# Squaring the log on ScalarE for even heads and on GpSimd for odd ones, in a hyperbolic attention kernel

## The reference

```python
q_hyp = _expmap0(qn); k_hyp = _expmap0(kn)
inner = -jnp.einsum('bhti,bhsi->bhts', q_hyp[..., :1], k_hyp[..., :1]) + jnp.einsum('bhtd,bhsd->bhts', q_hyp[..., 1:], k_hyp[..., 1:])
mdot = jnp.maximum(-inner, 1.0 + 1e-06)
dist = jnp.arccosh(mdot)
scores_hyper = -(dist * dist) / curv_k
scores = (1.0 - alpha) * scores_euclid + alpha * scores_hyper
scores = jnp.where(causal[None, None], scores, -jnp.inf)
attn = jax.nn.softmax(scores, axis=-1) * spike_mask
y = jnp.einsum('bhts,bhsd->bhtd', attn, v)
```

## Time and profile before

| | |
|---|---|
| median of 3 runs | 2524.64 us (2520.67 to 2529.24) |
| the profiled execution | 2528.54 us |
| its span, first to last instruction | 2526.8 us |
| mean granted TensorE clock | 0.835 |
| first stage, from about | 100 to 1130 us |

### The profile page before, as it was taken

One profiled execution on the slowest core, in us unless ns is written; L12 is line 12 of the kernel. 1 busy time (PEld: TensorE's weight loads), 2 busy tenths in 40 slices (PEclk: granted clock), 3 DMA queues, 4 the chain that ended last, 5 costly groups with the idle time before them and its releaser, 6 DMA issues. The chain is left out here.

```text
span 2526.8 us, 38830 instructions
## 1 busy us (share of the span) xinstructions
PE 2123.9 (84%) x12343; PEld 1132.9 (45%) x12344; DVE 1605.6 (64%) x3493; ACT 1493.4 (59%) x2762; POOL 613.4 (24%) x638
## 2 busy tenths in 40 slices
PE   4599899989898989994688988888885399999991
PEld 2244444545454444442222322222222288888880
DVE  4576877878787877672566556666652555555556
ACT  1487887888787878882156555565564143333332
POOL 4321314041413232014111122112012133333320
PEclk9677897979897968787689878887777599999995
DMA  1220202121211111100502222452434811111116
GB/s 46 71 64 17 79 18 63 39 59 43 59 43 55 47 51 43 34 9 17 84 18 43 43 51 68 109 143 79 108 108 144 331 67 44 48 44 48 46 38 208
DMA packets 140067, 172.35 MB, mean 68 GB/s; under 512 B 23874, under 2 KB 120339, under 8 KB 137875
## 3 DMA queue, kind: packets, MB, share of 16 engines
q1 hardware_dynamic: 131426, 149.58, 21.3%
q0 software_dynamic: 7488, 20.46, 2.7%
q10 hardware_dynamic: 1008, 0.54, 0.1%
HBM read 105.47 MB, written 65.01 MB: 67 GB/s over the span
## 5 line engine op out<-in xcount | busy, mean ns | idle before, releaser
L1243 DVE TENSOR_REDUCE NM<-sP 128x1 f32<-128x512 f32 x512 | 332.9, 684 | 241.5 <-PE sP L1126 239.6
L1058 ACT ACTIVATE PT<-tP 128x512 f32<-128x512 f32 x512 | 285.7, 604 | 264.9 <-PE tP L1138 263.0
L674 DVE CUSTOM_DVE_ANT_0 YZ<-SeP,YZ 128x512 f32<-128x512 f32 (+3 forms) x512 | 243.5, 487 | 196.4 <-PE SeP L541 179.2
L476 ACT ACTIVATE YZ<-YZ,gsc 128x512 f32<-128x512 f32 (+3 forms) x512 | 325.6, 663 | 69.4 <-DVE YZ L663 69.1
L1489 ACT ACTIVATE H<-hP,B1T 128x256 f32<-128x256 f32 x312 | 127.0, 473 | 271.0 <-PE hP L1568 209.0
L566 PE MATMUL tPa<-ident,YZ 128*128 128x128 f32 x1280 | 258.0, 323 | 1.2 <-ACT PTa L462 0.8
L454 ACT ACTIVATE XL<-mP 128x512 f32<-128x512 f32 (+1 forms) x384 | 204.9, 534 | 63.6 <-PE mP L551 63.3
L462 ACT ACTIVATE PTa<-tPa 128x512 f32<-128x512 f32 (+1 forms) x384 | 207.6, 541 | 41.9 <-PE tPa L572 37.7
L540 PE MATMUL SeP<-STG 48*128 48x512 f16 (+3 forms) x512 | 172.6, 337 | 50.7 <-DVE mn L674 49.5
L663 DVE SCALAR_TENSOR_TENSOR YZ<-YZ,XL 128x1280 f32<-128x1280 f32 x128 | 198.8, 1553 | 21.0 <-ACT YZ L468 19.6
L1126 PE MATMUL sP<-STGb 48*128 48x512 f16 x512 | 171.0, 449 | 46.2 <-DVE NM L1243 36.0
(11 more groups left out here) (301 smaller groups left out, 3994.4 us busy)
## 6 DMA issues: line engine op xcount, KB each, us to landing
STG<-planes_a_scratch SPq DMA_DIRECT2D x512, 32.0 KB, 1.9
X<-in_L_ffn_W SPq DMA_DIRECT2D x32, 512.0 KB, 4.2
weight_planes<-X SPq DMA_DIRECT2D x64, 256.0 KB, 2.5
STGb<-planes_scratch SPq DMA_DIRECT2D x96, 128.0 KB, 6.9
planes_a_scratch<-HI SPq DMA_DIRECT2D x64, 128.0 KB, 1.7
planes_a_scratch<-LO SPq DMA_DIRECT2D x64, 128.0 KB, 1.8
STG<-planes_a_scratch SPq DMA_DIRECT2D x128, 64.0 KB, 2.1
Y<-results_scratch SPq DMA_DIRECT2D x16, 512.0 KB, 8.8
```

Of the source, the lines that this page charges most:

```text
L476: act.activation(w, w, ACT.Square, bias=gsc[:, b % 2, 1, i, hh:hh + 1], scale=gsc[:, b % 2, 0, i, hh:hh + 1]).then_inc(hyp_ready, 1)
L674: dve.tensor_tensor_reduce(out=w, in0=SeP[tc % 2][:, 0:W[i]], in1=w, scale=1.0, scalar=3e38, op0=ALU.add, op1=ALU.min, accum_out=mn[:, h % ...
L1058: act.activation(PT[:, p % 4, par, kt, :], tP[x % 3][:, :], ACT.Exp).then_inc(exp_done, 1)
L1243: dve.tensor_reduce(NM[:, g % 2, col:col + 1], sP[n % 2][:, :], AX.X, ALU.max, negate=True).then_inc(max_done, 1)
```

## The change

Squares of even heads stay on ACT. Those of odd heads become a multiplication of `XL` by itself on POOL, in the same slot and with the same waits, ahead of whatever piece POOL has in that slot. The semaphore `y_ready` becomes two, one for each engine, and Z waits for the one of its head.

```diff
-            y_ready = sem("y_ready")
+            y_even = sem("y_even")
+            y_odd = sem("y_odd")
...
                 def _(pool):
                     for n in range(BEGIN, END):
                         s, t = n // SUB, n % SUB
+                        h = s - 1
+                        if t == 2 and 0 <= h < HEADS and h % 2 == 1:
+                            pool.wait_ge(clamped, h + 1)
+                            if h >= NYZ:
+                                pool.wait_ge(tp_full, 3 * (h - NYZ + 1))
+                            pool.tensor_tensor(YZ[:, h % NYZ, :], XL[:, h % NXL, :], XL[:, h % NXL, :], ALU.mult).then_inc(y_odd, 1)
...
                         h = s - 1
-                        if t == 2 and 0 <= h < HEADS:
+                        if t == 2 and 0 <= h < HEADS and h % 2 == 0:
                             act.wait_ge(clamped, h + 1)
                             if h >= NYZ:
                                 act.wait_ge(tp_full, 3 * (h - NYZ + 1))
-                            act.activation(YZ[:, h % NYZ, :], XL[:, h % NXL, :], ACT.Square).then_inc(y_ready, 1)
+                            act.activation(YZ[:, h % NYZ, :], XL[:, h % NXL, :], ACT.Square).then_inc(y_even, 1)
...
                         if t == 0 and 0 <= h < HEADS:
-                            dve.wait_ge(y_ready, h + 1)
+                            dve.wait_ge(y_odd if h % 2 else y_even, h // 2 + 1)
```

## The result

The changed kernel takes 2596.56 us, the median of 4 executions (2577.43 to 2602.07), against 2523.20 for the kernel before beside it (4, 2520.67 to 2529.24). The ratio is 1.0262 with an interval of 1.0221 to 1.0302: 73 us more, 2.6% slower. I had forecast 2530 and given "slower" 0.35.

What follows compares the result with a forecast made beforehand. PE was taken as near its limit in the hyperbolic attention, ACT often waiting for Z. Losses of 0.4 us a batch over 8 batches (3 us) plus 2 us in the last 20 heads gave +5: 2530 us, range 2512 to 2548.

Steps and rivals of the forecast that it cites:

- slower: Rival, chance 0.35: POOL's square makes Z late with thin cover; 2560 us uncovered in 8 batches, 2542 half covered.
- its rival: Rival "faster", chance 0.20: ACT's relief reaches PE in the hyperbolic attention, giving 10 to 26 us, 2499 to 2515.
- ACT's idle time before its cubic step: ACT's waits for Z before L476, 69 us, should grow by 40 us or more.
- The forecast of heads 72 and 73: From Z at 687.23 to Z at 700.89, 13.7 us; under 13.2 would prove the forecast wrong.
- Z at head 71: Behind a POOL piece, the square ends near 688.7, so Z starts at 688.75 and not 687.23, 1.5 us late.
- contention: DVE and POOL lengthen each other where the square meets L681: 0 to 0.65 us for each, 0.5 taken on the square.
- the cover: DVE or PE work between square and Z hides a Z later by up to about 1 us; other remainders cost nothing.
- PE's stop for ACT's copy: At head 71, PE's stop until 699.21 for the copy at 698.54 was to grow by 0.9 us.
- The stop for the combine of head 73: PE's stop at 703.56 was to shrink by 0.54 us, then lose 0.2 as Z ends 0.2 late.
- the late starts: Late Z starts at seven odd remainders, 4.4 us over one batch; uncovered in 8 batches 35 us.
- The signs that I set for it: For "slower": DVE's Z waiting for POOL in over 30 places, with PE's waits for DVE above 58 us.
- The watch that PE's busy 947 us would stay within 10: Core sign in the hyperbolic attention: PE's busy time stays within 10 us while ACT's idle time grows.

Runs made afterwards that it cites:

- the fill: Kernel before, with POOL at the first 55 odd heads filling 2688 unused columns with ones and reading nothing: 2530.35 us, ratio 0.9981.
- the kernel with five pieces: Changed kernel with POOL's square in five operations of 256 columns instead of one of 1280: 2575.48 us, ratio 1.0128 against the kernel before.
- the filler run: Changed kernel with two extra 512-column matmuls, result unread, before PE's wait in every second iteration: 2599.56 us, ratio 1.0238 against the kernel before.

## Why the prediction was wrong

**What held.** The square on POOL was priced at 2.35 us and took 2.32; the Trainium skill's figure (GPSIMD Engine Reference, Performance versus the Vector engine), from which I had estimated 2.8, is too high for this form. That figure is for an add of two inputs, where the square reads one tensor twice. The trace of before has a case of either: L1032, two different inputs of 512 f32 columns, has a median of 1.27 us where L400 has 1.04. The relief of ACT was sized at 10 to 26 us in its rival and is worth 13. ACT's idle time before its cubic step was to grow by 40 us or more and grew by 73. The forecast of heads 72 and 73, not under 13.2 us, also held: they take 14.2.

**What came right by luck.** Z at head 71 was to start 1.5 us late; seen from the clamp's end it is 1.35 us late (4.51 against 3.16). But I had the square slowed to 2.9 us and DG to about 1.1. In fact the square kept its 2.32 us and DG stood beside it, ending 0.54 us behind: the sum is the same, the mechanism is not. In the same way DG was to be near 1.1 us at odd heads. Its mean there is 1.15, made of 30 cases at about 0.69 us and 33 that were held, up to 2.76.

**The step that failed first: contention.** I bounded it at 0 to 0.65 us by the longest DG, 1.34 us in the earlier trace rows, and called the upper end a full overlap. It was not even that: those DGs began 0.37 us into a POOL instruction of 1.16 us and ended 0.55 us after it. What a DG pays is what is left of the POOL instruction when it begins, and beside an instruction of 2.32 us that was up to 2.07 us more than usual. The evidence was in the trace of before, in the ends and not in the lengths. The clamp at head 73 there takes 1.38 us and not 0.82. It starts at 696.76, beside this instruction of POOL:

```profile
696.30 1.16 POOL L428 TENSOR_TENSOR LO<-QFa,HI 128x512 f16<-128x512 f32 x1
```

POOL ends at 697.46 and the clamp at 698.14, 0.68 us later, with nearly its whole work still to do after POOL's end. A shared resource that slowed both would not look so. I put 0.5 on the square, which in fact kept its length in 62 of 64 cases (2.75 and 2.77 us in the other two): DVE took nearly all of it. In the stretch, DVE's busy time grew by 44 us, 0.7 an odd head. DG has 26 of them; most of the rest are small operations that come once a batch behind a clamp, above all L769, 2.22 us beside the square and 0.22 before (L762 there).

The Trainium skill says this outright (SBUF — State Buffer, SBUF: two separate sides): the interfaces that VectorE and GpSimd share are "an **exclusive lock**, not a bandwidth split", for the whole instruction, against a VectorE operation with two SBUF inputs when GpSimd reads, or one in a 2-port mode. The runs agree: DG and Z are held and the combine, which has one input in PSUM, is not (0.67 to 0.69 us for its 512 columns in every kernel); the fill, which only writes, leaves DG at 0.69 us. The clamp and the `TENSOR_SCALAR` of 0.22 us have one input and are held too, the latter even by the fill, which would fit the 2-port mode; in which mode they ran, no trace shows. The four long DGs of the kernel with five pieces, held past the end of one instruction, go beyond what it says. It was the rule that spoke against this change, and I didn't use it.

**The step that failed second, and weighs more: the cover, and the clock put at nothing.** Head 71 was to lose 0.1 us, heads 73 and 77 0.2 and 0.1, the other remainders nothing, by work lying between Z and PE's need of it; the sum was 5 us. PE's stop for ACT's copy was to grow from 0.55 us by 0.9 and stayed at 0.57 (747.79 above). The stop for the combine of head 73 was to shrink by 0.54 and then lose 0.2: it grew from 0.54 to 1.64. I had Z of head 73 end only 0.2 us late. From the clamp's end (746.58) to Z's end (752.57) are 5.99 us where there were 4.75 before, 1.24 us late, since DG was held for 1.82 us and Z itself was lengthened again, to 2.18.

The rival "slower", with all of the late starts uncovered, gave 35 us. Even that is half of what came, and so are its late starts: from the clamp's end to Z's start, the 64 odd heads together need 70 us more than before, part of it because PE is slower, as at head 75. The signs that I set for it did not appear: Z waited for POOL once and not in over 30 places, and PE's waits for DVE grew from 49.5 to 52.5 us and not over 58. PE's idle time in the stretch grew by 6 us. All my terms were stops of PE, and there was no term for a PE that runs slower. The watch that PE's busy 947 us would stay within 10 was the one that broke: 1017. That is 70 of the 76 us, and they came with the clock, 0.84 to 0.77.

The runs show the link from DVE's delay to the clock by its two ends: two ways of delaying DVE (POOL's reading, DG made twice) lower the clock, and taking DG out of POOL's way brings 0.77 back to 0.84. They don't show what in PE's work makes the chip grant less; the filler run spoke against the gap in front of that one wait.

**What stays open.** Why DVE's time is dear at about 1.5 to 1.7 us of stretch for each us in front of Z (65/42 and 76/44), and why still 0.8 or more behind it (37/45 by the windows), when DVE is busy for only 795 of 1029 us. The chain DVE to ACT to DVE to PE leaves its idle time scattered where it can't be used; that is argued from the waits, not shown.

## What to carry to other kernels

When work goes to POOL, the price is paid by DVE: look at what two-input SBUF operations DVE has while the POOL instruction runs, and charge the first of them the whole remaining length of it (DG here: 0.69 us became up to 2.76); then move either of them. When a trace shows a few instances of an operation at twice the usual time, compare their ends with the end of what ran beside them before taking the longest as a bound. And before pricing ACT relief, ask what a microsecond of each engine is worth in this loop: here one of DVE's in front of Z cost more than one, and reordering a single DVE operation behind Z, with no change of engine, gave 0.8 to 1.3%.

## What the runs showed of the hardware

- A DVE operation that is held by POOL ends a fixed time after POOL does, however long it has stood: 0.54 to 0.55 us for every DG that began in a square, as at 736.22 above, and 0.68 to 0.69 us for the clamps held in the kernel before. The profile shows it as busy from its start, and no wait appears.
- The hold works both ways. At head 71 the low-half split on POOL took 2.28 us and not 1.15, since Z had begun before it (736.15, ending at 738.04) and it ended 1.01 us after Z. The timeline of POOL there:

```profile
735.62 1.07 POOL L433 CAST HI<-QFa 128x512 f16<-128x512 f32 x1
736.77 2.28 POOL L435 TENSOR_TENSOR LO<-QFa,HI 128x512 f16<-128x512 f32 x1
```

- A held DVE operation does not always get in between two POOL instructions that follow each other at once: 3.22 and 4.93 us for DG in the kernel with five pieces, where it had begun 0.07 and 0.06 us before the end of a piece.
- The granted clock of a stretch moved from 0.84 to 0.77 with the same instructions on PE and 6 us more of idle time in 1105, and PE's busy time grew by 70 us. After the stop of 1.64 us at head 73 PE ran at full clock to 755.8 and then at half clock to 762.6.
